# Post-LN decoder: the second layer's key/value side re-cut and moved to pairs 5 to 7, the VectorE division moved behind the second clamp and the score slot

## The chip, the cores and the metric

One core of one Trainium2 chip. The metric is the device time of one execution in microseconds; the kernel before has a median of 1208.59 us over 3 runs (1207.61 to 1209.77).

## The reference, cut to what matters

Two decoder layers over `x` (8 batches of 256 rows of 128) with a context `ctx_1024` (8 batches of 512 rows of 128). The first layer is a windowed self-attention with 16 heads of 8, a cross-attention with 16 heads of 64 (rotary keys, scores clipped to ±11) and a quantised product. The second layer is a recurrence over 256 steps, a linear cross-attention and an fp8-like product. What the change touches is the division of the first layer's cross-attention and the key/value side of the second layer's:

```python
# first layer, cross-attention
attn = softmax(clip(q @ k.T * scale, -11, 11))      # 16 heads, in 8 pairs
out  = attn @ v

# second layer, linear cross-attention: key/value side
kh = _split_heads(_layernorm(ctx @ wk, ln_gamma, ln_beta))     # eps 1e-6
vh = _split_heads(_layernorm(ctx @ wv, ln_gamma, ln_beta))
k_prime = (relu(kh) + 1e-6) * mask
vh = vh * mask
kv = einsum('bhnd,bhne->bhde', k_prime, vh)          # and k_prime.sum over the rows
```

Only the 128 by 128 product of `k_prime` with `vh`, and the column sums of `k_prime`, leave this side; they are kept per batch in `kv_sums`, and the last stage of the kernel reads them.

## The kernel before, in words

The program has a queue of its own for each engine, and each queue is written out in the order in which it executes; the engines meet through semaphores.

**Three parts.** First a setup with the self-attention of batch 0, for which no other work runs beside it (0 to about 87 us). Then a loop over the batches b = 0 to 7, in each of which the cross-attention of batch b runs as 8 pairs of heads, and the self-attention of batch b+1 is dealt out between its steps in 48 slots, 6 to a pair (`PER_PAIR`, `S_...`, lines 57 to 67; slot s belongs to pair s // 6). The last batch has pairs without slots. Then the rest of both layers, from about 868 us on: the recurrence and what follows, which the change leaves alone but for the width of one tile.

**A pair.** TensorE (`batch` under `block.tensor`, `unit` at line 1572): `unit(0)` makes half the scores in the two score banks, then the keys' first product for the pair after next, slot 0, then `values_of(pair - 1)` (L1544) and `sum_of(pair - 1)` (L1552) into `out_bank`, slot 1, `unit(1)` into the same score banks, and then the queries' product, slots and the other products ("prep" jobs, L1358 to L1360) in turns. ScalarE: `exps(0)`, slots 0 and 1, `exps(1)` (L776), then queries, slots and values evacuations (L738). VectorE (`batch`, lines 1075 to 1105): `keys_job("a")` (k_cos, L1010), `clamp(0)` (L1078), slots 0 and 1, `attended(pair - 1)` (reciprocal L1050 and product L1051), `clamp(1)`, slot 2, `keys_job("b")` (k_sin, L1012), slots 3 and 4 and 5. GpSimd: slots 0 and 1, two of three additions of the clamped values (L614, L616), slots 2 and 3, the third (L618), slot 4, `rotate` (L590), slot 5.

**What waits for what.** `values_of` of the next pair and, at the end of pair 0, `output` of the batch before (L1527, 32 matmuls) wait for `on_ready`, which `attended` gives. `unit(1)` waits for `exps(0)`, and the `unit(0)` after it for `exps(1)` and the queries' evacuation. The prep jobs go through one or two banks: in pairs 1 and 5 the second values job, in pair 3 (one bank only) the first, waits until `keys_job("b")` has emptied the bank. `bank_a` is a single bank that ScalarE empties, in the order of the jobs `A_X` to `A_LAT` (lines 70 to 71); `bank_d` the same for VectorE. A score slot (L1428) waits until VectorE has read the scores before it (L939, L941).

**The second layer's key/value side, for batch b+1.** Slot 3 (pair 0): TensorE turns the context into `bank_a` (L1339, from `cb`), ScalarE copies it to `ctx_t`. Slots 5 and 6: two products each of 128x256 with `w_l1kv` (L1417), each half copied by ScalarE to `kv1` (L670, 128x512). Slots 9 and 13: VectorE takes mean and variance of four tiles of `kv1` (`measure`, L885, L888), GpSimd makes scale and bias (`scale_and_bias`, L548 to L551). Slots 10 and 15: ScalarE normalises four tiles in place (L678). Slots 17 to 20: GpSimd multiplies by `l1_g` and adds `l1_b`, two halves of 128x512 each (L572). Slot 23: VectorE makes relu, value times mask, key times mask (L960 to L962). Slot 40: TensorE makes the product (L1464, 4 matmuls of 128x129), VectorE copies it (L993).

```python
                if slot in S_NORM:
                    k = S_NORM.index(slot)
                    tiles = tiles_of(kv1[:, KB * k:KB * (k + 1), :], KB)
                    dve.wait_ge(a_free, n(b, ACT_JOBS, SETUP_A + A_KV + k + 1))
                    dve.wait_ge(rstd_ready, norms + 1 + k)
                    measure(tiles, 1)
```

## Time and profile before

| | us |
|---|---|
| median of 3 runs | 1208.59 |
| the profiled execution: time | 1209.53 |
| its span, first to last instruction | 1207.7 |
| setup and self-attention of batch 0 | 0 to 88.2 |
| loop, batches 0 to 6 (with slots), one each | 100.0, 100.5, 100.9, 101.9, 100.0, 101.3, 100.0 |
| last batch (no slots) | 69.4 |
| the rest | 345.5 |
| PE / DVE / ACT / POOL busy | 991.9 (82%) / 686.5 (57%) / 520.4 (43%) / 484.0 (40%) |

Read the stages first: a mean over them says nothing of a change that moves work within one iteration of the loop. A pair's stage is measured here from its first score matmul (`unit(0)`) to the next pair's, so that its length is what TensorE spends on it. PE is TensorE, DVE VectorE, ACT ScalarE, POOL GpSimd.

### The profile page before, as it was taken

What the parts mean: (1) busy time and instruction counts of PE and PEld (TensorE: products, weight loads), DVE (VectorE), ACT (ScalarE), POOL (GpSimd) and SP (SyncE); (2) the same over time, 40 slices, a digit from 0 to 9 for tenths busy, and PEclk for the clock granted to TensorE, in tenths of its full rate; (3) what the DMA queues carried; (4) which work ended last, traced back from release to release, by engine and by line L of the source; (5) the groups of instructions that cost most, each with busy time, mean ns of one, the idle gap of its engine ahead of it and who ended that gap; (6) DMA issues with size and microseconds to landing.
All of it is one profiled execution on the core that took longest, in us unless ns stands there. A gap on an engine that the chain in (4) does not pass through costs nothing.

```text
span 1207.7 us, 19775 instructions
## 1 busy us (share of the span) xinstructions
PE 991.9 (82%) x7491; PEld 664.9 (55%) x7491; DVE 686.5 (57%) x1895; ACT 520.4 (43%) x1414; POOL 484.0 (40%) x553
## 2 busy tenths in 40 slices
PE   4578899899799979989979998998746999996311
PEld 3355566566566656656756665665434755663311
DVE  2535666566656666666765767654474002445498
ACT  3726545564664465556466446532211233331000
POOL 1224555546455554654645555465421000111031
PEclk8779899799999989989998999999956999997655
DMA  6000000000000000000000000000000000010401
GB/s 167 18 3 13 1 1 14 1 1 6 10 1 1 14 2 1 14 1 1 6 10 1 1 1 1 1 19 1 1 1 1 2 1 4 8 8 3 52 0 35
DMA packets 56813, 12.85 MB, mean 11 GB/s; under 512 B 40318, under 2 KB 56462, under 8 KB 56590
## 3 DMA queue, kind: packets, MB, share of 16 engines
q1 hardware_dynamic: 56718, 11.58, 4.7%
q8 instruction: 60, 0.98, 0.3%
q14 instruction: 35, 0.29, 0.1%
HBM read 9.46 MB, written 2.12 MB: 10 GB/s over the span
## 4 chain that ended last, share of the span: by engine, by line
PE 58%; DVE 23%; ACT 10%; POOL 3%; issue 3%; DMA 2%; SPq 1%; POOLq 0%; DVEq 0%
PE score_banks L1572 8%; PE out_bank L1544 8%; PE bank_d L1670 6%; PE bank_a L1339 5%; DVE o_rec L1050 5%; PE score_banks L1734 4%; PE score_banks L1358 4%; DVE prob L1078 3%; ACT prob L716 3%; PE score_banks L1383 3%; DVE stats L885 3%; PE out_bank L1527 3%; PE score_banks L1360 2%; PE score_banks L1359 2%; PE out_bank L1552 2%
## 5 line engine op out<-in xcount | busy, mean ns | idle before, releaser
L776 ACT ACTIVATE prob<-score_banks 128x1024 f32<-128x1024 f32 x128 | 130.8, 1022 | 154.5 <-PE score_banks L1572 154.1
L1572 PE MATMUL score_banks<-qh,kr 64*128 64x256 f32 x1024 | 153.2, 420 | 6.2 <-ACT prob L776 4.9
L616 POOL TENSOR_TENSOR psum<-psum,prob 128x512 f32<-128x512 f32 x64 | 81.6, 1274 | 166.1 <-DVE prob L1078 166.1
L539 POOL TENSOR_TENSOR var_eps<-mv,epsilons 128x2 f32<-128x2 f32 (+2 forms) x64 | 12.6, 197 | 335.6 <-DVE mv L888 335.4
L1050 DVE RECIPROCAL o_rec<-out_bank 128x256 f32<-128x256 f32 x64 | 111.8, 1747 | 32.9 <-PE out_bank L1552 32.9
L1544 PE MATMUL out_bank<-prob,v 128*64 128x256 f32 x1024 | 124.6, 385 | 1.3 <-DVE on L1051 1.3
L614 POOL TENSOR_TENSOR psum<-prob 128x512 f32<-128x512 f32 x64 | 82.3, 1286 | 99.5 <-DVE prob L1078 99.5
L1572 PEld LDWEIGHTS score_banks<-qh,kr 64*128 64x128 f32 x1024 | 92.8, 195 | 45.4 <-issue 26.6
L1078 DVE TENSOR_SCALAR prob<-prob 128x1024 f32<-128x1024 f32 x128 | 101.2, 790 | 26.9 <-ACT prob L776 26.9
L1010 DVE TENSOR_TENSOR k_cos<-score_banks,cos_t 128x512 f32<-128x512 f32 x56 | 38.6, 690 | 123.0 <-POOL kr L590 75.4
L716 ACT ACTIVATE prob<-prob,neg_max 128x128 f32<-128x128 f32 (+1 forms) x256 | 106.4, 420 | 0.0
L1670 PE MATMUL bank_d<-w_qkv_t,ident 128*64 128x192 f32 (+1 forms) x430 | 105.9, 332 | 0.0
L1428 PE MATMUL bank_d<-km,q 64*128 64x128 f32 (+1 forms) x512 | 60.9, 361 | 47.3 <-DVE row_max L941 46.7
L1339 PE MATMUL bank_a<-ident,prob 128*128 128x128 f32 x400 | 73.8, 315 | 27.4 <-DMA prob<-att_scratch 17.4
L1544 PEld LDWEIGHTS out_bank<-prob,v 128*64 128x64 f32 x1024 | 67.8, 136 | 46.8 <-issue 17.4
L827 ACT ACTIVATE prob<-score_banks 128x8 f32<-128x8 f32 x255 | 45.2, 177 | 104.9 <-PE score_banks L1734 103.6
L590 POOL TENSOR_TENSOR kr<-k_cos,k_sin 128x512 f32<-128x512 f32 x64 | 82.8, 1293 | 10.3 <-DVE k_sin L1012 10.3
L618 POOL TENSOR_TENSOR psum<-psum,prob 128x512 f32<-128x512 f32 x64 | 81.5, 1273 | 3.4
L1734 PEld LDWEIGHTS score_banks<-prob,pt 128*64 128x64 f32 x1020 | 52.2, 134 | 54.6 <-ACT prob L827 48.6
L670 ACT ACTIVATE pt<-bank_a 128x512 f32<-128x512 f32 x96 | 57.0, 594 | 55.2 <-PE bank_a L1339 55.2
L1339 PEld LDWEIGHTS bank_a<-ident,prob 128*128 128x128 f32 x400 | 50.9, 158 | 53.0 <-DMA prob<-att_scratch 17.9
L1734 PE MATMUL score_banks<-prob,pt 128*64 128x8 f32 x1020 | 75.3, 212 | 0.7 <-ACT prob L827 0.3
(352 smaller groups left out, 2035.6 us busy)
## 6 DMA issues: line engine op xcount, KB each, us to landing
cb<-in_ctx_dram SPq DMA_DIRECT2D x8, 256.0 KB, 2.9
bias_mask<-bias_scratch SPq DMA_DIRECT2D x1, 1536.0 KB, 7.5
xb<-in_x_dram SPq DMA_DIRECT2D x8, 128.0 KB, 2.2
prob<-in_L_xattn_Wkv_dram SPq DMA_DIRECT2D x1, 1024.0 KB, 6.8
att_scratch<-on SPq DMA_DIRECT2D x16, 64.0 KB, 3.1
prob<-att_scratch SPq DMA_DIRECT2D x2, 512.0 KB, 4.1
out_dram<-v SPq DMA_DIRECT2D x4, 256.0 KB, 2.3
prob<-in_L_xattn_Wq_dram SPq DMA_DIRECT2D x1, 512.0 KB, 8.1
```

What stands on the lines that cost most here:

```text
L590: g.tensor_tensor(kr[:, key % 2, :], k_cos[:, :], k_sin[:, :], ALU.add).then_inc(kr_ready, 1)
L614: link(g.tensor_tensor(psum[:, p % 2, :], pp[:, 0, :], pp[:, 1, :], ALU.add))
L616: link(g.tensor_tensor(psum[:, p % 2, :], psum[:, p % 2, :], pp[:, 2, :], ALU.add))
L716: last = s.activation(pr, pr, ACT.Exp, bias=neg_max[:, qt, j, g:g + 1], accum_out=row_sum[:, qt, j, g:g + 1])
L776: s.activation(prob[:, p % 2, 2 * u:2 * u + 2, :].rearrange("p k (h q) -> p h k q", h=2), sc[:, 0:2, :].rearrange("p h (k q) -> p h k q", ...
L1050: link(w.reciprocal(o_rec[:, :], bank[:, T:2 * T]))
L1078: w.tensor_scalar(pr, pr, float(np.exp(-CLIP)), float(np.exp(CLIP)), ALU.max, ALU.min).then_inc(clamped, 1)
L1339: return nc.tensor.transpose(out_ap, in_ap, ident[0:in_ap.shape[0], 0:in_ap.shape[0]])
L1544: mm(o[DH * h:DH * (h + 1), 0:T], v[:, (q // 2) % 2, kb, lo:lo + DH], prob[:, q % 2, kb, T * h:T * (h + 1)], start=(kb == 0), stop=(kb == ...
L1572: last = mm(sc[:, h, k * T:(k + 1) * T], kr[rows_of, p % 2, kb * P:(kb + 1) * P], qh[rows_of, p % 2, :], start=True, stop=True, skip_group ...
L1670: mm(bank_d2[0:HALF_ROWS, 0:columns], ident[:, 0:HALF_ROWS], w_qkv_t[:, 0:columns], start=True, stop=True, skip_group_check=True)
L1734: last = mm(cf[lo:lo + HALF_ROWS, t * B:(t + 1) * B], a_t[:, lo:lo + HALF_ROWS], hid[:, (t - 1) * B:t * B], start=False, stop=True, skip_g ...
```

## The change

It does two things.

**One.** The second layer's key/value side is computed otherwise. The weights `w_l1kv` are centred once at the start on VectorE (2 statistics, 2 aggregations, 2 subtractions), so that a row of the product has mean zero and needs a scale alone. `kv1` is gone: VectorE measures the product in `bank_a` itself, GpSimd makes the scale (add, power, times a mask factor: 3 operations in place of 4), and ScalarE writes each of the four tiles of a half scaled out of `bank_a` into `k1` or `v1` (4 activations of 128x128 in place of one copy of 128x512 and 4 activations). GpSimd's gain and bias are applied to `k1` alone (2 operations in place of 4), VectorE's relu too (1 in place of 3); the values' gain and bias are applied to the 128x128 product, with one column more in the matmul (128x130) and three VectorE operations in place of one copy.

**Two.** All of it moves: the context's turning from slot 3 to 34, the two halves of the product from slots 5 and 6 to 35 and 39, the statistics with them on VectorE, GpSimd's scale to slots 36 and 40, ScalarE's evacuation to 37 and 41, gain and bias to 42 and 43, relu to 44, the last product from slot 40 to 47. And in every pair `attended` comes behind `clamp(1)` and slot 2.

```diff
-S_X, S_K, S_Q, S_CTX, S_V, S_KV_A, S_KV_B = range(7)
+S_X, S_K, S_Q, S_CTX, S_V = range(5)
-S_CTX_NORM, S_NORM, S_KV_NORM, S_AFFINE, S_RELU = 5, (9, 13), (10, 15), (17, 18, 19, 20), 23
-S_SUMS, S_REC, S_DIVIDE, S_PROJ, S_X1, S_LATN, S_KV, S_LAT = 29, 33, 34, 35, 37, 38, 40, 43
+S_CTX_NORM = 5
+S_SUMS, S_REC, S_DIVIDE, S_PROJ, S_X1, S_LATN, S_LAT = 29, 33, 34, 35, 37, 38, 43
+S_TURN_CTX, S_KV, S_KV_SCALE, S_KV_OUT = 34, (35, 39), (36, 40), (37, 41)
+S_AFFINE, S_RELU, S_KV_SUM = (42, 43), 44, 47
-A_X, A_K, A_CTX, A_KV, A_CN, A_TURN, A_REC, A_LAT = 0, 1, 2, 3, 5, 6, 18, 19
+A_X, A_K, A_CN, A_TURN, A_REC, A_CTX, A_KV, A_LAT = 0, 1, 2, 3, 15, 16, 17, 19
...
 # GpSimd
+                if slot in S_KV_SCALE:
+                    half = S_KV_SCALE.index(slot)
+                    scale = act_scale[:, 1 + half, :]
+                    if half == 0:
...
+                        g.tensor_copy(v1[:, :, D:D + 2], keep_pair[:, b, :, :])
+                    pool.wait_ge(kv_var_ready, n(b, 2, half + 1))
+                    link(g.tensor_tensor(var_eps[:, 4:8], mv[:, 4:8, 1], epsilons[:, EPSILONS.index(1e-6), 4:8], ALU.add))
+                    link(g.tensor_tensor(scale, var_eps[:, 4:8], minus_half[:, 4:8], ALU.pow))
+                    g.tensor_tensor(scale, scale,
+                                    kv_factor[:, b, 2 * half:2 * half + 2, :].rearrange("p k t -> p (k t)"),
+                                    ALU.mult).then_inc(kv_scale_ready, 1)
                 if slot in S_AFFINE:
+                    first = slot == S_AFFINE[0]
+                    if first:
+                        pool.wait_ge(a_free, n(b, ACT_JOBS, SETUP_A + A_KV + 2))
+                    row, op = (l1_g, ALU.mult) if first else (l1_b, ALU.add)
+                    last = g.tensor_tensor(k1[:, :, :], k1[:, :, :], row[:, :].unsqueeze(1).broadcast_to([P, KB, D]), op)
...
 # ScalarE
+                if slot in S_KV_OUT:
+                    half = S_KV_OUT.index(slot)
+                    act.wait_ge(kv_scale_ready, n(b, 2, half + 1))
+                    if half == 0 and b >= 1:
+                        act.wait_ge(d_free, n(b, DVE_JOBS, SETUP_D))
+                    for i in range(4):
+                        dst = (k1[:, 2 * half + i // 2, :], v1[:, 2 * half + i // 2, 0:D])[i % 2]
+                        last = s.activation(dst, bank_a[:, i * D:(i + 1) * D], ACT.Identity,
+                                            scale=act_scale[:, 1 + half, i:i + 1])
+                    last.then_inc(a_free, 1)
-                if slot == S_CTX:
+                if slot == S_TURN_CTX:
+                    act.wait_ge(cn_split, b + 1)
                     evacuate(b, A_CTX, ctx_t[:, :], bank_a[:, :])
-                if slot in (S_KV_A, S_KV_B):
-                    evacuate(b, A_KV + k, kv1[:, 4 * k:4 * k + 4, :].rearrange("p k d -> p (k d)"), bank_a[:, :])
...
 # VectorE
+                if slot in S_KV:
+                    half = S_KV.index(slot)
+                    dve.wait_ge(a_full, n(b, ACT_JOBS, SETUP_A + A_KV + half + 1))
+                    if half == 1:
+                        dve.wait_ge(kv_scale_ready, n(b, 2, 1))
+                    measure(tiles_of(bank_a[:, :].rearrange("p (k d) -> p k d", d=D), 4), 1, kv_var_ready)
                 if slot == S_RELU:
                     dve.wait_ge(kv_ready, n(b, 1, 1))
-                    link(w.tensor_scalar(k1[:, :, :], kv1_v[:, :, 0, :], 0.0, 1e-6, ALU.max, ALU.add))
-                    w.tensor_tensor(v1[:, :, 0:D], kv1_v[:, :, 1, :], keep_b, ALU.mult)
-                    w.tensor_tensor(k1[:, :, :], k1[:, :, :], keep_b, ALU.mult).then_inc(k1_ready, 1)
+                    w.tensor_scalar(k1[:, :, :], k1[:, :, :], 0.0, 1e-6, ALU.max, ALU.add).then_inc(k1_ready, 1)
-                if slot == S_KV:
+                if slot == S_KV_SUM:
                     bank_ready(b, D_KV)
-                    w.tensor_copy(kv_sums[:, b, :], bank_d[:, 0:D + 1]).then_inc(d_free, 1)
+                    w.tensor_copy(kv_sums[:, b, D:D + 2], bank_d[:, D:D + 2])
+                    link(w.tensor_tensor(kv_sums[:, b, 0:D], bank_d[:, 0:D], l1_g[:, :], ALU.mult))
+                    w.scalar_tensor_tensor(out=kv_sums[:, b, 0:D], in0=l1_b[:, :], scalar=kv_sums[:, b, D + 1:D + 2],
+                                           in1=kv_sums[:, b, 0:D], op0=ALU.mult, op1=ALU.add).then_inc(d_free, 1)
...
                     clamp(0)
                     slots(0, 1)
                     slots(1, 2)
+                    clamp(1)
+                    slots(2, 3)
                     if pair >= 1:
                         attended(pair - 1)
-                    clamp(1)
-                    slots(2, 3)
                     keys_job("b")
...
 # TensorE
-                if slot == S_CTX:
+                if slot == S_TURN_CTX:
                     pe.wait_ge(ctx_in, n(b, 16, 16))
                     a_job(A_CTX)
-                if slot in (S_KV_A, S_KV_B):
+                if slot in S_KV:
...
-                if slot == S_KV:
+                if slot == S_KV_SUM:
                     bank = d_job(D_KV)
                     pe.wait_ge(k1_ready, n(b, 1, 1))
                     for kb in range(KB):
-                        last = mm(bank[:, 0:D + 1], k1[:, kb, :], v1[:, kb, :], start=(kb == 0), stop=(kb == KB - 1))
+                        last = mm(bank[:, 0:D + 2], k1[:, kb, :], v1[:, kb, :], start=(kb == 0), stop=(kb == KB - 1))
```

On SyncE the load of the next context follows the context's turning (`a_free` of `A_CTX`), and so moves from pair 0 to pair 5.

## Rows read from the trace of the kernel before

**Rows 1.** Busy time by pair of one iteration: stage, length, PE, PEld, DVE, ACT, POOL, clock

```profile
288.70:302.40 13.70, 13.46 (x98) 10.41 (x97) 8.16 (x19) 6.38 (x13) 9.77 (x11) 1.00 0.04 11
302.40:317.30 14.90, 12.67 (x92) 8.86 (x91) 10.98 (x43) 7.36 (x14) 4.84 (x7) 0.97 0.07 19
317.30:336.80 19.50, 15.12 (x98) 9.46 (x97) 11.02 (x46) 13.24 (x43) 12.84 (x16) 0.76 0.00 1
336.80:351.00 14.20, 13.75 (x119) 9.16 (x118) 9.89 (x25) 8.37 (x25) 8.01 (x7) 1.00 0.00 1
...
361.20:373.10 11.90, 11.90 (x101) 8.39 (x99) 7.05 (x9) 5.54 (x11) 5.97 (x6) 1.00 0.00 0
373.10:380.60 7.50, 7.50 (x56) 5.11 (x55) 6.48 (x16) 2.60 (x4) 4.23 (x7) 1.00 0.01 3
380.60:389.60 9.00, 8.90 (x62) 5.82 (x61) 7.17 (x11) 4.54 (x7) 5.34 (x5) 1.00 0.00 0
```

**Rows 2.** Timeline of pairs 1 and 2: start, duration, engine, line, idle before and releaser

```profile
314.97 0.82 PE L1428 MATMUL bank_d<-km,q 64*128 64x128 f32 x8 [2.09 <-DVE row_max L941]
315.20 0.68 DVE L1012 TENSOR_TENSOR k_sin<-score_banks,sin_t 128x512 f32<-128x512 f32 x1
...
317.26 2.08 PE L1572 MATMUL score_banks<-qh,kr 64*128 64x256 f32 x8
...
319.11 1.65 ACT L678 ACTIVATE kv<-kv,act_bias,act_scale 128x128 f32<-128x128 f32 x4 [5.58 <-POOL act_bias L551]
...
328.80 1.68 DVE L1078 TENSOR_SCALAR prob<-prob 128x1024 f32<-128x1024 f32 x1
...
331.60 1.44 PE L1428 MATMUL bank_d<-km,q 64*128 64x128 f32 x8 [3.91 <-DVE row_max L941]
```

**Rows 3.** Busy time of lines over that iteration: count, busy us, mean ns, idle before

```profile
L1050 DVE RECIPROCAL o_rec<-out_bank 128x256 f32<-128x256 f32 x8 | 14.0, 1747 | 3.9 <-PE out_bank L1552 3.9
L1078 DVE TENSOR_SCALAR prob<-prob 128x1024 f32<-128x1024 f32 x17 | 13.5, 792 | 2.7 <-ACT prob L776 2.7
...
L572 POOL TENSOR_TENSOR kv<-kv,l_g 128x512 f32<-128x512 f32 x2 | 2.5, 1272 | 0.1
...
L678 ACT ACTIVATE kv<-kv,act_bias,act_scale 128x128 f32<-128x128 f32 x8 | 3.3, 482 | 7.3 <-POOL act_bias L551 7.3
...
L549 POOL TENSOR_TENSOR act_scale<-var_eps,minus_half 128x4 f32<-128x4 f32 x3 | 3.1, 1017 | 0.2
...
L1417 PE MATMUL bank_a<-w_l1kv,ctx_t 128*128 128x256 f32 x8 | 2.2, 392 | 0.2 <-ACT ctx_t L670 0.2
...
L885 DVE BATCH_NORM_STATS2 stats<-kv 128x6 f32<-128x128 f32 x8 | 1.7, 276 | 0.0
...
L1464 PE MATMUL bank_d<-v,k 128*128 128x129 f32 x8 | 1.1, 274 | 0.0
```

**Rows 4.** Timeline of pairs 0, 3, 5, 6 and 7 around the division

```profile
294.98 1.02 ACT L776 ACTIVATE prob<-score_banks 128x1024 f32<-128x1024 f32 x1 [0.69 <-PE score_banks L1572]
...
298.71 0.49 PE L1527 MATMUL out_bank<-wo,on 128*128 128x128 f32 x3
...
343.57 1.02 ACT L776 ACTIVATE prob<-score_banks 128x1024 f32<-128x1024 f32 x1 [3.30 <-PE score_banks L1572]
...
347.42 0.39 PE L1358 MATMUL score_banks<-wv_s,cn_s 128*128 128x256 f32 x1 [0.24 <-DVE k_sin L1012]
...
370.44 0.69 DVE L1012 TENSOR_TENSOR k_sin<-score_banks,sin_t 128x512 f32<-128x512 f32 x1 [0.68 <-PE score_banks L1360]
...
378.56 1.03 ACT L776 ACTIVATE prob<-score_banks 128x1024 f32<-128x1024 f32 x1 [3.24 <-PE score_banks L1572]
...
385.23 1.13 PE L1572 MATMUL score_banks<-qh,kr 64*128 64x256 f32 x8
```

**Rows 5.** Chain that ended last, before the loop: start, duration, engine, line

```profile
69.41 0.73 PE bank_d L1456 x4
...
78.43 0.77 PE score_banks L1358
```

More of the change, by code:

```diff
@@ L279, in decoder @@
         x2 = sb("x2", [P, NT, D])
-        kv_sums = sb("kv_sums", [P, B, D + 1])
+        kv_sums = sb("kv_sums", [P, B, D + 2])
         mats = km[:, :, :].rearrange("p j t -> p (j t)").rearrange("p (k d) -> p k d", d=D)
@@ L542, in rstd_of, with scale_and_bias @@
                                 ALU.pow).then_inc(done, 1)
-            def scale_and_bias(before, k, eps):
-                scale, bias = act_scale[:, k, :], act_bias[:, k, :]
-                pool.wait_ge(var_ready, before + k + 1)
-                link(g.tensor_tensor(var_eps[:, 4:8], mv[:, 4:8, 1], epsilons[:, EPSILONS.index(eps), 4:8], ALU.add))
+            def scale_and_bias(before):
+                scale, bias = act_scale[:, 0, :], act_bias[:, :]
+                pool.wait_ge(var_ready, before + 1)
+                link(g.tensor_tensor(var_eps[:, 4:8], mv[:, 4:8, 1], epsilons[:, 0, 4:8], ALU.add))
                 link(g.tensor_tensor(scale, var_eps[:, 4:8], minus_half[:, 4:8], ALU.pow))
@@ L672, in evacuate, with apply_norm @@
                     i.then_inc(a_free, 1)
-            def apply_norm(norms, k, dst, src):
-                act.wait_ge(rstd_ready, norms + k + 1)
-                for i in range(4):
-                    last = s.activation(dst[:, i, :], src[:, i, :], ACT.Identity, scale=act_scale[:, k, i:i + 1],
-                                        bias=act_bias[:, k, i:i + 1])
+            def apply_norm(norms):
+                act.wait_ge(rstd_ready, norms + 1)
+                for i in range(KB):
+                    last = s.activation(cn[:, i, :], cb[:, i, :], ACT.Identity, scale=act_scale[:, 0, i:i + 1],
+                                        bias=act_bias[:, i:i + 1])
                 return last
@@ L875, in _ @@
             w.tensor_copy(cos_t[:, :], bank_d[:, :]).then_inc(d_free, 1)
+            for half in range(2):
+                w.bn_stats(stats[:, half, :], w_l1kv[:, half * D:(half + 1) * D])
+            link(w.memset(stats[:, 2, 0:1], 0.0))
+            for half in range(2):
+                w.bn_aggr(mv[:, half, :], stats[:, half, :])
+            link(w.memset(stats[:, 2, 0:1], 0.0))
+            for half in range(2):
+                tile = w_l1kv[:, half * D:(half + 1) * D]
+                last = w.tensor_scalar(tile, tile, mv[:, half, 0:1], None, ALU.subtract)
+            last.then_inc(kv_centred, 1)
             def band_of(h, count):
@@ L1411, in self_attention @@
                     last.then_inc(d_full, 1)
-                if slot in (S_KV_A, S_KV_B):
-                    j = slot - S_KV_A
+                if slot in S_KV:
+                    j = S_KV.index(slot)
+                    if b == 0:
+                        pe.wait_ge(kv_centred, 1)
                     a_job(A_KV + j)
```

69 lines of the change are left out of this document (28 added, 41 removed).

## The prediction

> **What bounds the kernel now.** I read the busy time by pair first [rows 1]. Seven of the 48-slot iterations make up 705 of the 1207.7 us, so the question is what one of them becomes. In pairs 5 to 7 (and in pair 4, left out of the rows) TensorE is busy for the whole stage at full clock: these are bound by its work. Pairs 1 and 2 are not: pair 2 takes 19.5 us for 15.12 of TensorE, at a granted clock of 0.76, and 15.12 x 0.76 = 11.5 is what it would need at full clock. The timeline says why [rows 2]: TensorE waits 2.09 and 3.91 us for VectorE to read scores, and ScalarE waits 5.58 us for GpSimd's scale of the key/value side before its four activations, with the exponentials of pair 2 queued behind them. So an iteration has slack of two kinds: TensorE's idle time in pairs 1 and 2, which the change attacks, and VectorE's and ScalarE's idle time in pairs 4 to 7, which it wants to use. The second kind is worth something only if the new steps there don't form a chain that TensorE waits for.
>
> **The change part by part**, for one iteration, each number against the lengths of [rows 1].
>
> *Pair 2, 19.5 to 12.2: -7.3.* The chain measure (1.3: four statistics of 0.28 overlapping, four aggregations), GpSimd's four operations (1.9, of which the power is 1.02 [rows 3]), ScalarE's 1.65 [rows 2] leaves the path to the first exponential; a second measure of 1.3 leaves VectorE, and the slot's scores come ahead of the division, so that the 3.91 us wait goes. I take TensorE's own 11.5 plus 0.7 of leftover waits.
>
> *Pair 1, 14.9 to 14.0: -0.9.* Half the product leaves (2.2 us for both halves [rows 3], 0.9 of queue pace each). The wait of 2.09 us changes its cause instead of going: the second values job needs `k_sin` out of its bank, and k_sin stood at 315.20, the job right behind it [rows 2]. VectorE still has to do the exponential's clamp, the scores, the division and k_sin in a row, after the second exponential, whose time is TensorE's doing. I get k_sin at the same time after the stage's start, within 0.4.
>
> *Pair 0, 13.7 to 14.1: +0.4.* The other half of the product and the turning leave (1.3). But the second exponential ends at 296.0 [rows 4]; the division (a reciprocal of 1.75 [rows 3] and a product, 2.2 in all) used the wait for it and was over by then. Now it comes behind it: clamp 0.7, slot 2's scaling of the queries 0.4, division 2.2, so 299.4 with the starts. TensorE's output of the batch before, which needs this division, began at 298.71 [rows 4] and, with 1.3 us less ahead of it, could begin at 297.4. It waits 2, and ends 0.4 later than before after all; the GpSimd and VectorE steps behind it have their 2 us of idle time to take that in.
>
> *Pair 3, 14.2 to 16.4: +2.2.* The same, with a price one can read off: the first values job waits for k_sin already now (0.24 at 347.42, rows 4), k_sin follows the division, and the division leaves the gap in front of the exponential that ends at 344.6. It shifts by its whole 2.2. That GpSimd's four additions and VectorE's mask products (3.8 us at the pair's end) go is worth nothing: they ran beside TensorE's work, and k_sin was ahead of them.
>
> *Pair 4: 0.* k_sin is late by 1.7, but its bank is needed in pair 5 only.
>
> *Pair 5, 11.9 to 13.5: +1.6.* Turning 0.45 and half a product 0.9 come in; k_sin moves from 370.44 [rows 4] to about 372.0, which delays the second values job by 0.3.
>
> *Pairs 6 and 7, 16.5 to 24.2: +7.7.* The heart of the matter. Time runs from pair 6's first score matmul. VectorE measures half A (1.3) ahead of the projection's sum, so GpSimd has done the projection's scale only at 3.3 and half A's (a copy and three operations, 1.9) at 5.2; ScalarE's four activations (4 x 0.41 = 1.65) stand ahead of the second exponential and end at 6.9, so that one ends at 7.95 (was 6.5: 378.56 + 1.03, rows 4). Call this E. From there one chain has to run before the first exponential of pair 7, which is queued on ScalarE behind half B's activations: clamp 0.7, latent norm 0.6, division 2.2, k_sin 0.7, measure B 1.3, GpSimd 1.7, ScalarE 1.65, exponential 1.05: E + 10. Pair 7's `unit(1)` starts at 17.9; it started at 12.1 (385.23, rows 4). That is +5.8. Then TensorE has values 1.5, and needs GpSimd's gain and bias (2 x 1.27 [rows 3]) and relu for the last product; relu sits behind the second clamp and ends 3.6 after `unit(1)`'s start; product 1.05 [rows 3], queries 0.55, keys 0.9, in all 6.2 against 4.4. +1.9. TensorE idles some 5 us in this stretch. The turning of the latents waits as well, since it needs `bank_a` from half B; it is ready before `unit(1)` all the same.
>
> *The clock: +2.* After the idle 2.09 us the eight score matmuls of pair 2 took 2.08 against 1.13 us elsewhere [rows 2, 4], and the stage shows 0.76 [rows 1]; the granted clock was at its lower level, 1.2 GHz. One such stretch costs TensorE about 1.7 us. My lengths for pairs 1 and 2 assume full clock, which takes out what they lost; but there are now idle stretches of 2 us or more in pairs 0, 1, 3 and 7. Between 0 and 4 x 1.7 = 6.8; in the trace not each wait of 2 us was followed by a fall, so I take 2.
>
> Sum: -7.3 - 0.9 + 0.4 + 2.2 + 1.6 + 7.7 + 2 = +5.7 for an iteration, times 7: **+40**.
>
> *Ahead of the loop: +8.* Two passes of ScalarE's four activations (3.2) leave the chain of exponentials. But between the projection (69.41) and the first prep job (78.43) [rows 5] ran 9.0 us of latents; now both halves of the key/value side, A, then B, then gain, bias, relu and product run there, with nothing beside them: from the projection's old time 1.7 (half A ahead of it), 1.3 measure, 2.2 the projection's sum and scale, 2.5 GpSimd, 1.65, half B 0.9 + 1.3 + 1.7 + 1.65, and 5 for gain, bias, relu and product: 20 in place of 9.0, and 20 - 9 - 3.2 = 7.8. Centring the weights (some 1.6 us) hides in VectorE's idle time before 17 us.
>
> *Last batch: +11.* No slots, so pairs are short, and the division's 2.2 us comes right before what needs it: it ends 2.9 after the second exponential (clamp 0.7, division 2.2), where the next pair's values can start 2.0 after it (scores 1.1, keys 0.9), and k_sin is 2.2 later where a values job waits for it. Pair 0 3.2 (the output, with a clock loss); pairs 1, 3 and 5, where the wait is for k_sin, 2.1, 1.0 and 1.9, the second less as TensorE's keys are late there already; pairs 2, 4 and 6 0.6, 0.6 and 1.5; the last division 1.2, as GpSimd's sum was late already. Of these 12 I take 11.
>
> *At nothing:* the one column more in the matmul, the load of the context (needed only at the next pair 0), three VectorE operations for `kv_sums` (1.0 in place of 0.3, beside GpSimd's rotation, for which VectorE waits there).
>
> **A rule beside the rows.** The clamp took 1.68 us at 328.80 [rows 2] against a mean of 0.79 [rows 3]; GpSimd's addition L614 ran beside it. The Trainium skill (SBUF — State Buffer, the shared port pair) has it that VectorE and GpSimd take that pair in turns for a whole instruction, the loser blocked. By that the two additions and the mask products saved would free VectorE, which speaks for the change; and relu and clamp of pair 7 would meet GpSimd's additions, which were ahead of them, which speaks against it by 0.8 to 1 us an iteration. My sum has neither.
>
> **It comes to** 1209.5 (the profiled execution; its span is 1207.7) + 40 + 8 + 11 = 1268.5; the median is 0.9 below that execution: **1267.6 us**.
>
> **The rivals.** (a) *Faster.* VectorE and ScalarE get to the division and to half B in time, and only the gain of pairs 0 to 3 stands: then these need TensorE's work alone, by busy time times clock in [rows 1] 51.0, less the 2.2 moved 48.8, in place of 62.3 us. With pairs 5 to 7 at my price (+9.3) that is -4.2 an iteration: 1208.6 - 29 + 8 + 11 = 1199; were only the 2.2 us of moved work added there, 1208.6 - 79 + 19 = 1149. For it: VectorE idles a third of the iteration. Against: the waits are for one instruction in a fixed order, and the exponential's end is TensorE's doing, not VectorE's. The point from which it decides is half B's last activation: done by 11.0 us after pair 6 began it delays nothing (12.1 less an exponential); I sum 17. The queue order is the same in every iteration, so it would be all seven or none. 0.10. (b) *Half hidden.* The chain from E is 3 to 4 us shorter than summed (its waits overlapping with what I put behind one another): 21 to 28 us less, about 1240 to 1247; 0.2. (c) *All idle stretches lose the clock*: +4.8 an iteration, 1301; also if SBUF contention adds: 0.12. (d) *No change.* The gain in pair 2 larger by 3 and the chain shorter by 3, about 1212 to 1205: 0.03. (e) The move does not take place, since something ties the slots: no; each queue is written in order. My forecast itself has 0.55.
>
> **How the numbers follow.** Over 0.2% (about what a measurement of this kernel can tell from no change) slower are the forecast, (b) and (c): 0.87. The range: no clock loss (-14) and (b) together give 1226, and I go some way on towards (d), to 1218, as (a) and (d) lie outside with 0.13; above, (c) gives 1300.
>
> **What would show it.** Right: pair 2 near 12 us and the wait before ScalarE's activations gone there; ScalarE waiting 2 us and more for GpSimd's scale in pairs 6 and 7, and the first exponential of pair 7 about 10 us after the second of pair 6; a wait of TensorE's output for the division in pair 0; in pair 3 a wait of 2 us for k_sin; iterations of about 106 us. Wrong: pairs 6 and 7 together under 19 us, or pairs 0 to 3 together under 52.

## The result, and the profile after

The changed kernel takes **1272.9 us** (median of 4 runs, 1269.43 to 1276.43) against 1209.18 for the kernel before beside it: **1.053 times as long, 95% interval 1.0506 to 1.0557**. It was forecast at 1267.6, in a range of 1218 to 1300, and slower with 0.87. The profiled execution spans 1268.4 us, so 60.7 have to be found against the 1207.7 of before. VectorE, ScalarE and GpSimd are busy for less than before (682.5, 504.8 and 467.7 us), and TensorE's work is the same but for its clock.

Busy time by pair of the iteration that answers to [rows 1]; its columns are stage, length, then PE, PEld, DVE, ACT and POOL busy with their counts, granted clock, DMA share and GB/s:

```profile
300.10:314.40 14.30, 12.11 (x88) 9.23 (x87) 9.46 (x21) 4.68 (x9) 6.40 (x10) 1.00 0.04 11
314.40:328.30 13.90, 11.34 (x86) 7.74 (x85) 10.62 (x40) 8.27 (x18) 7.96 (x8) 1.00 0.00 1
328.30:341.70 13.40, 11.79 (x101) 7.64 (x99) 8.41 (x34) 9.41 (x31) 5.53 (x5) 1.00 0.01 2
341.70:358.00 16.30, 13.72 (x121) 9.14 (x119) 7.07 (x23) 8.49 (x26) 5.09 (x4) 1.00 0.01 1
...
368.10:381.80 13.70, 13.70 (x112) 9.77 (x109) 7.48 (x12) 6.42 (x12) 6.81 (x6) 1.00 0.02 5
381.80:389.20 7.40, 7.40 (x50) 4.75 (x49) 4.94 (x21) 3.36 (x7) 4.97 (x10) 1.00 0.10 31
389.20:407.40 18.20, 12.80 (x68) 8.47 (x67) 13.49 (x21) 5.46 (x11) 12.45 (x12) 0.82 0.00 0
```

Pair 2 went from 19.5 to 13.4 us and back to full clock; pair 7 doubled, with 5.4 us in which TensorE does nothing, at a granted clock of 0.82. Iterations differ by some us, so I count with the mean of each pair over batches 0 to 6 from here on:

| us | before | after | difference |
|---|---|---|---|
| pair 0 | 12.92 | 13.69 | +0.8 |
| pair 1 | 15.23 | 14.32 | -0.9 |
| pair 2 | 19.33 | 13.44 | -5.9 |
| pair 3 | 14.88 | 16.32 | +1.4 |
| pair 4 | 10.17 | 10.17 | 0 |
| pair 5 | 11.94 | 13.61 | +1.7 |
| pairs 6 and 7 | 16.46 | 24.46 | +8.0 |
| sum, times 7 batches | | | +36 |
| first pair starts | 86.29 | 93.79 | +7.5 |
| from batch 7's pair 0 to the end | 414.9 | 432.4 | +17.5 |

36 + 7.5 + 17.5 = 61: that is the whole difference (60.7, unrounded). The timeline of pairs 6 and 7 shows the chain (pair 6 begins at 381.76):

```profile
386.72 0.37 ACT L710 ACTIVATE k<-bank_a,act_scale 128x128 f32<-128x128 f32 x1 [2.75 <-POOL act_scale L583]
...
387.74 1.04 ACT L797 ACTIVATE prob<-score_banks 128x1024 f32<-128x1024 f32 x1
...
388.81 1.32 DVE L1108 TENSOR_SCALAR prob<-prob 128x1024 f32<-128x1024 f32 x1 [2.22 <-ACT prob L797]
...
390.05 1.59 DVE L931 TENSOR_SCALAR lat<-x,mv,rstd 128x128 f32<-128x128 f32 x2
...
391.57 1.74 DVE L1080 RECIPROCAL o_rec<-out_bank 128x256 f32<-128x256 f32 x1
391.64 1.26 POOL L636 TENSOR_TENSOR psum<-psum,prob 128x512 f32<-128x512 f32 x1
393.35 0.42 DVE L1081 TENSOR_TENSOR on<-out_bank,o_rec 128x256 f32<-128x256 f32 x1
393.69 0.68 DVE L1044 TENSOR_TENSOR k_sin<-score_banks,sin_t 128x512 f32<-128x512 f32 x1
...
393.82 3.45 PE L1576 MATMUL out_bank<-prob,v 128*64 128x256 f32 x16 [2.58 <-DVE on L1081]
...
397.26 0.37 ACT L710 ACTIVATE k<-bank_a,act_scale 128x128 f32<-128x128 f32 x1 [8.21 <-POOL act_scale L583]
...
399.37 1.13 PE L1604 MATMUL score_banks<-qh,kr 64*128 64x256 f32 x8 [0.47 <-ACT prob L797]
...
403.90 1.67 PE L1496 MATMUL bank_d<-v,k 128*128 128x130 f32 x8 [1.77 <-DVE k L991]
```

Read it from ScalarE: it waits 2.75 us for the scale of half A and 8.21 for that of half B, and `unit(1)` of pair 7 starts behind it at 399.37, 17.6 us after pair 6 began (it was 12.1 before, [rows 4]). TensorE has a second wait of its own, 2.58 us at 393.82, for the division, and the sixteen value matmuls behind it take 3.45 us. The same sixteen take 1.95 where the clock is granted in full, as in the next fence. The other waits for VectorE, in pairs 0, 1 and 3 and in the last batch's last two value steps and output:

```profile
310.66 3.84 PE L1559 MATMUL out_bank<-wo,on 128*128 128x128 f32 x32 [2.19 <-DVE on L1081]
327.45 0.38 PE L1388 MATMUL score_banks<-wv_s,cn_s 128*128 128x256 f32 x1 [2.28 <-DVE k_sin L1044]
354.39 0.38 PE L1388 MATMUL score_banks<-wv_s,cn_s 128*128 128x256 f32 x1 [2.37 <-DVE k_sin L1044]
...
913.76 1.95 PE L1576 MATMUL out_bank<-prob,v 128*64 128x256 f32 x16 [1.40 <-DVE on L1081]
921.18 3.68 PE L1576 MATMUL out_bank<-prob,v 128*64 128x256 f32 x16 [3.98 <-DVE on L1081]
928.03 6.16 PE L1559 MATMUL out_bank<-wo,on 128*128 128x128 f32 x30 [2.32 <-DVE on L1081]
```

Why VectorE is late though it works less stands in one row of the costliest groups, the clamps. They wait 165.9 us for the exponentials in the whole kernel:

```profile
L1108 DVE TENSOR_SCALAR prob<-prob 128x1024 f32<-128x1024 f32 x128 | 102.5, 801 | 165.9 <-ACT prob L797 165.1
```

The row of the kernel before, for the same 128 clamps:

```profile
L1078 DVE TENSOR_SCALAR prob<-prob 128x1024 f32<-128x1024 f32 x128 | 101.2, 790 | 26.9 <-ACT prob L776 26.9
```

The other 139 us of waiting were filled by the division, done while VectorE would have waited anyway. The experiments below bear this out: the same row shows 21.4 us of waiting with the division back in its place (experiment 1) and 157.8 with the division alone moved (experiment 2).

### The profile page after: what moved, and what is told of

It reads as the page before. It is cut to its first block, busy times and chain, and to the rows that moved or that the text cites. A ratio compares the mean times of both kernels' runs of the same rounds, so it can differ in the third digit from the quotient of the medians.

```text
span 1268.4 us, 19745 instructions
## 1 busy us (share of the span) xinstructions
PE 990.2 (78%) x7491; PEld 664.3 (52%) x7491; DVE 682.5 (54%) x1903; ACT 504.8 (40%) x1398; POOL 467.7 (37%) x532
## 4 chain that ended last, share of the span: by engine, by line
PE 53%; DVE 25%; ACT 11%; issue 4%; POOL 3%; DMA 2%; SPq 1%; POOLq 0%; DVEq 0%; ACTq 0%
PE score_banks L1604 8%; PE out_bank L1576 7%; PE bank_d L1702 6%; DVE o_rec L1080 6%; ACT prob L797 5%; PE bank_a L1369 4%; PE score_banks L1766 4%; PE out_bank L1559 3%; PE score_banks L1388 3%; DVE stats L917 3%; DVE prob L1108 3%; PE score_banks L1413 2%; ACT prob L737 2%; PE out_bank L1584 2%; PE score_banks L1390 2%
## 5 line engine op out<-in xcount | busy, mean ns | idle before, releaser
L1108 DVE TENSOR_SCALAR prob<-prob 128x1024 f32<-128x1024 f32 x128 | 102.5, 801 | 165.9 <-ACT prob L797 165.1
L1576 PE MATMUL out_bank<-prob,v 128*64 128x256 f32 x1024 | 136.0, 412 | 24.5 <-DVE on L1081 24.5
L1604 PE MATMUL score_banks<-qh,kr 64*128 64x256 f32 x1024 | 148.0, 408 | 5.0 <-ACT prob L797 3.7
L1604 PEld LDWEIGHTS score_banks<-qh,kr 64*128 64x128 f32 x1024 | 89.9, 189 | 44.1 <-issue 29.3
L1576 PEld LDWEIGHTS out_bank<-prob,v 128*64 128x64 f32 x1024 | 71.9, 144 | 75.1 <-DVE on L1081 29.2
L1369 PE MATMUL bank_a<-ident,prob 128*128 128x128 f32 x400 | 66.7, 291 | 25.5 <-DMA prob<-att_scratch 17.2
L636 POOL TENSOR_TENSOR psum<-psum,prob 128x512 f32<-128x512 f32 x64 | 81.3, 1270 | 4.5
L1369 PEld LDWEIGHTS bank_a<-ident,prob 128*128 128x128 f32 x400 | 46.3, 146 | 47.6 <-DMA prob<-att_scratch 17.7
L1388 PE MATMUL score_banks<-wv_s,cn_s 128*128 128x256 f32 x112 | 36.8, 328 | 40.1 <-DVE k_sin L1044 39.1
```

Source lines behind the costliest of these rows:

```text
L1108: w.tensor_scalar(pr, pr, float(np.exp(-CLIP)), float(np.exp(CLIP)), ALU.max, ALU.min).then_inc(clamped, 1)
L1369: return nc.tensor.transpose(out_ap, in_ap, ident[0:in_ap.shape[0], 0:in_ap.shape[0]])
L1576: mm(o[DH * h:DH * (h + 1), 0:T], v[:, (q // 2) % 2, kb, lo:lo + DH], prob[:, q % 2, kb, T * h:T * (h + 1)], start=(kb == 0), stop=(kb == ...
L1604: last = mm(sc[:, h, k * T:(k + 1) * T], kr[rows_of, p % 2, kb * P:(kb + 1) * P], qh[rows_of, p % 2, :], start=True, stop=True, skip_group ...
```

## The experiments

The change has two parts that can be undone apart. **Theory A**: each has a price, the division's place where TensorE waits for the division or for `k_sin`, the key/value side's place in pairs 6 and 7. **Theory B**: most of it is the chain of the key/value side alone. Each kernel was timed beside the kernel before.

**1. The division back in its place, the rest of the change kept**

```diff
                     slots(1, 2)
+                    if pair >= 1:
+                        attended(pair - 1)
                     clamp(1)
                     slots(2, 3)
-                    if pair >= 1:
-                        attended(pair - 1)
```

> The changed kernel with the division back ahead of the second clamp; the key/value side stays in pairs 5 to 7. Theory A (two prices: the division's place and the late key/value chain, each with its own): the waits for the division in pair 0 and for k_sin in pair 3 go (2.2 us each), pair 5 loses 0.4, pairs 6 and 7 fall from 24.5 to about 22 since the division runs in the wait for the second exponential again, and the last batch gets its 16 us back; an iteration takes about 98 us and the whole about 1200. Theory B (the late key/value chain is what makes the kernel slower, the division is mostly hidden): less than 25 us come back, the whole stays above 1245.

1201.52 us, 0.9936 of before (0.991 to 0.9961). Theory A. By pair against the changed kernel: pair 0 -2.6, pair 3 -2.1, pair 2 -1.0, pairs 6 and 7 -1.1, in all -6.9 an iteration; from the last batch on -19.5. Undoing the place of the division gives back 67 us of span, more than the 61 lost. The key/value side as changed is, alone, **6.7 us faster than before** by the spans of the profiled executions, 5.8 by the medians (-1.8 an iteration, +7.8 ahead of the loop, -2 at the end), though half B's chain is all there:

```profile
374.21 0.37 ACT L710 ACTIVATE k<-bank_a,act_scale 128x128 f32<-128x128 f32 x1 [2.75 <-POOL act_scale L583]
...
382.63 0.37 ACT L710 ACTIVATE k<-bank_a,act_scale 128x128 f32<-128x128 f32 x1 [6.09 <-POOL act_scale L583]
...
384.74 2.08 PE L1604 MATMUL score_banks<-qh,kr 64*128 64x256 f32 x8 [0.48 <-ACT prob L797]
```

Pair 6 began at 369.25 here: `unit(1)` of pair 7 starts 15.5 us later, 2.1 less than in the changed kernel, but its eight matmuls take 2.08 us instead of 1.13. Part of what the shorter chain gave went to the clock. Pairs 6 and 7 still take 23.4 us in the mean, 6.9 more than before: in these two pairs the late chain is a real loss, which the 8.7 us gained over pairs 0 to 5 outweigh.

**2. The division late, the key/value side as before**

The same move, in the kernel before.

> The kernel before with the division alone moved behind the second clamp and slot 2. Theory A: pair 3 +2.2, pair 0 +0.7, pair 5 +0.7, pair 6 +0.6, pair 2 shorter by up to 2 as its scores come ahead of the division; some +2 us an iteration and +16 in the last batch, so about 1240. Theory B: within 10 us of the kernel before.

1276.15 us, 1.0579 (1.0536 to 1.0623): the direction of theory A, but 36 us past its number. The division alone costs 66 us of span here, 67 on top of the new key/value side: over the whole kernel the two parts add up, and the loss is the division's. What I had missed is pair 7, +3.7 us with no key/value chain in it, and a clock lost in pair 3 as well (+2.8):

```profile
399.47 3.40 PE L1544 MATMUL out_bank<-prob,v 128*64 128x256 f32 x16 [2.40 <-DVE on L1051]
```

So in the changed kernel, too, the wait for the division in pair 7 would be there without the wait for half B; they lie side by side, and taking away either brings only part. Pairs 6 and 7 take 16.5 us with neither, 20.1 with the division late, 23.4 with the new key/value side and 24.5 with both: here both together cost 2.6 us less than their sum, in pair 0 they cost 2.0 more.

**3 and 4. Half B's activations behind the first exponential of pair 7 (slot 42), with what follows; then with the division back as well**

```diff
-S_SUMS, S_REC, S_DIVIDE, S_PROJ, S_X1, S_LATN, S_LAT = 29, 33, 34, 35, 37, 38, 43
-S_TURN_CTX, S_KV, S_KV_SCALE, S_KV_OUT = 34, (35, 39), (36, 40), (37, 41)
-S_AFFINE, S_RELU, S_KV_SUM = (42, 43), 44, 47
+S_SUMS, S_REC, S_DIVIDE, S_PROJ, S_X1, S_LATN, S_LAT = 29, 33, 34, 35, 37, 38, 44
+S_TURN_CTX, S_KV, S_KV_SCALE, S_KV_OUT = 34, (35, 39), (36, 40), (37, 42)
+S_AFFINE, S_RELU, S_KV_SUM = (43, 44), 44, 47
```

> The changed kernel with half B's activations behind pair 7's first exponential (slot 42), gain and bias at slots 43 and 44, and the latents' turning at slot 44. Theory A: pair 7's second scores no longer wait for half B; they start when the division has let the values through, some 3 to 4 us earlier; the last product then waits for gain, bias and relu, which gives back 1 to 2. Pairs 6 and 7 together 21.5 to 23 in place of 24.5, the whole about 1255 to 1262. Rival: the wait turns into one of the last product for relu of the same length, and nothing is gained (1270).

1318.59 us, 1.0897 (1.0853 to 1.0942): far above the range expected, and above the rival's 1270. The profiled execution is the shortest of the four (1309.04). Pairs 6 and 7 take 28.3 us. The wait for half B's scale did not go, it became a longer one behind it, in the timeline of pair 7:

```profile
407.03 1.95 PE L1576 MATMUL out_bank<-prob,v 128*64 128x256 f32 x16 [2.58 <-DVE on L1081]
...
416.65 1.26 POOL L592 TENSOR_TENSOR k<-k,l_b 128x512 f32<-128x512 f32 x1
417.95 1.47 DVE L991 TENSOR_SCALAR k<-k 128x512 f32<-128x512 f32 x1 [3.83 <-POOL k L592]
...
419.56 2.07 PE L1496 MATMUL bank_d<-v,k 128*128 128x130 f32 x8 [6.07 <-DVE k L991]
```

In slot 44 GpSimd's second operation stands behind two of its additions, which wait for the second clamp; relu waits for it, and behind relu stand the division and `k_sin`.

> As the run before, and the division back ahead of the second clamp. Theory A: pairs 6 and 7 together about 19 to 20, the rest as in the run with the division back; 96 us an iteration, about 1185 in all, faster than the kernel before. Rival: no better than with the division back alone (1200).

1246.37 us, 1.0317 (1.0294 to 1.034), missed by 61 us for the same reason: pairs 6 and 7 take 27.2 us, 3.8 more than in experiment 1, pairs 1 and 2 together 2.4 more.

**5 and 6. Half B one slot earlier, activations in slot 40; then with the division back as well**

```diff
-S_TURN_CTX, S_KV, S_KV_SCALE, S_KV_OUT = 34, (35, 39), (36, 40), (37, 41)
+S_TURN_CTX, S_KV, S_KV_SCALE, S_KV_OUT = 34, (35, 38), (36, 39), (37, 40)
```

> The changed kernel with half B one slot earlier: product and measure at slot 38 (ahead of the division and k_sin), scale at 39, activations at 40. Theory A: ScalarE is done with half B some 4 us earlier, but the division, now behind a measure too, holds the values of pair 6 about 1 us longer, and pair 7's second scores cannot start before them; pairs 6 and 7 together 23.5 to 25 (24.5 before), the whole 1265 to 1277. Theory B (the key/value chain sets pair 7): 3 us less an iteration, about 1252.

1275.63 us, 1.0538 (1.0481 to 1.0595). The total lies in theory A's range, but not by its mechanism, and that is luck: pairs 6 and 7 gained 2.2 us (22.3, where theory A had 23.5 to 25), most of theory B's 3, and pairs 0 to 3, which the edit does not touch, lost 2.9. The traces show where: TensorE is idle in pairs 0 to 3 for as long as in the changed kernel (8.9 and 9.0 us), but the granted clock (length times one less the clock) withholds 4.3 us there in place of 0.8. So this run does not show that half B's place is worth nothing.

> As the run before, with the division back ahead of the second clamp. Theory A: now the chain over half B alone sets pair 7's second scores, and it is shorter by division and k_sin's places: they start at about 13.6 us after pair 6 began in place of 15.5, and the clock is not lost; 2 to 3 us less an iteration than with the division back alone, about 1184. Rival: no change against that run (1201), since something else, such as GpSimd's queue, ends last.

1220.77 us, 1.0088 (1.007 to 1.0106): missed, and 18 us of span slower than experiment 1. Of these, 6 are in pairs 6 and 7 (24.3 us against 23.4), 11 again in pairs 0 to 2 (2.1 us an iteration withheld by the clock, 0.5 in experiment 1). `unit(1)` came earlier (13.7 us after pair 6 began), but the time was handed to the next wait:

```profile
386.82 1.74 DVE L1080 RECIPROCAL o_rec<-out_bank 128x256 f32<-128x256 f32 x1
388.60 0.42 DVE L1081 TENSOR_TENSOR on<-out_bank,o_rec 128x256 f32<-128x256 f32 x1
388.94 0.68 DVE L1108 TENSOR_SCALAR prob<-prob 128x1024 f32<-128x1024 f32 x1
389.54 0.42 DVE L991 TENSOR_SCALAR k<-k 128x512 f32<-128x512 f32 x1
...
390.11 2.07 PE L1496 MATMUL bank_d<-v,k 128*128 128x130 f32 x8 [3.88 <-DVE k L991]
```

Relu (L991) has its input 2.9 us before it starts, but stands behind the division and the second clamp in VectorE's queue.

**7. The new key/value side, the division back in pairs 0, 3 and 6 only** (the edit is shown against experiment 1)

```diff
+                    early = p in (0, 3, 6)
-                    if pair >= 1:
+                    if early and pair >= 1:
                         attended(pair - 1)
                     clamp(1)
                     slots(2, 3)
+                    if not early and pair >= 1:
+                        attended(pair - 1)
```

> The changed kernel with the division back ahead of the second clamp in pairs 0, 3 and 6 only, the last batch too. Theory A: only these three places cost TensorE much in the loop, 2.5, 2.1 and 1.1 us an iteration, some 40 us in all, and in the last batch some 8 of its 17; about 1225. The other pairs keep what they have. Rival: the price is spread over all pairs and less than half of 71 us comes back (above 1240).

1228.66 us, 1.0148 (1.0132 to 1.0164), near the 1225 expected: three of eight places give back 44 of the 71 us. What is left is pair 2 (15.4 us at a lower clock, 12.5 in experiment 1) and the last batch, 9 us longer. Pair 2 is a fourth place that costs, against the expectation; it is made up for in part by pairs 6 and 7, which take 22.3 us here and 23.4 in experiment 1.

**8. The kernel before, with the division late in pair 2 alone**

```diff
-                    if pair >= 1:
+                    early = p != 2 or last
+                    if early and pair >= 1:
                         attended(pair - 1)
                     clamp(1)
                     slots(2, 3)
+                    if not early and pair >= 1:
+                        attended(pair - 1)
```

> The kernel before with the division moved in pair 2 alone (not in the last batch), the one pair that came out shorter when it was moved everywhere (18.65 against 19.33). Theory A: pair 2 shorter by 0.7 to 2 us, 5 to 14 us less in all, 1194 to 1203. Rival: what pair 2 gains goes again in pair 3, no difference.

1205.91 us (9 runs), 0.9965 (0.9952 to 0.9979): faster, by less than expected. Pair 2, where TensorE waited 3.91 us for scores behind the division [rows 2], is the one pair that the move made shorter in the kernel before, and there it is worth 0.8 us.

**9. The smaller key/value side in the old place, the division in its old place**

The gain in pair 2 could come from the work being smaller or from its being gone. This run leaves it in pairs 0 to 3 (the edit is shown against experiment 1; two waits at its new places are left out).

```diff
-S_CN = 7
+S_CN = 11
...
-S_TURN_CTX, S_KV, S_KV_SCALE, S_KV_OUT = 34, (35, 39), (36, 40), (37, 41)
-S_AFFINE, S_RELU, S_KV_SUM = (42, 43), 44, 47
+S_TURN_CTX, S_KV, S_KV_SCALE, S_KV_OUT = 3, (5, 8), (5, 8), (6, 9)
+S_AFFINE, S_RELU, S_KV_SUM = (17, 18), 23, 40
...
-A_X, A_K, A_CN, A_TURN, A_REC, A_CTX, A_KV, A_LAT = 0, 1, 2, 3, 15, 16, 17, 19
+A_X, A_K, A_CTX, A_KV, A_CN, A_TURN, A_REC, A_LAT = 0, 1, 2, 3, 5, 6, 18, 19
```

> The smaller key/value side in pairs 0 to 3 instead of 5 to 7, the division ahead of the second clamp as before. Slots: context turned in 3, products in 5 and 8, GpSimd's scale in 5 and 8, ScalarE's activations in 6 and 9, gain and bias in 17 and 18, relu in 23, last product in 40; the turning of the normalised context moves from slot 7 to 11. Theory A (the change mixes a gain, fewer operations in pair 2, with two costs of its own: the place of the division and the place of the key/value side): this keeps the gain and neither cost. By pair, from the run with the division back: pair 0 11.1 and 1.3 for turning and half a product, pair 1 14.2 and 1.1, pair 2 12.5 to 13, pair 3 14.2, pair 4 10.2, pair 5 11.9, pairs 6 and 7 16.5 as before: about 93 us an iteration in place of 98.9, and the first pair some 8 us earlier: 1145 to 1170 us. Rival B (pair 2 got shorter because the work left it, not because it is smaller; in pairs 0 to 2 ScalarE again waits for GpSimd's scale ahead of the exponentials): pairs 0 to 2 together near 47 as before, 1185 us or more.

1179.09 us, 0.9737 (0.9708 to 0.9766): theory A in kind, short of its number. Pairs 0 to 2 take 41.8 us (47.5 before), pairs 5 to 7 what they took before, 95.1 in all. But the first pair starts at 97.2 us, 10.9 later than before. GpSimd's timeline ahead of the loop says why:

```profile
21.19 0.20 POOL L556 TENSOR_TENSOR act_bias<-act_bias,minus_one 128x4 f32<-128x4 f32 x1
33.27 0.24 POOL L574 TENSOR_TENSOR kv_factor<-keep 128x32 f32<-128x32 f32 x1 [11.88 <-DMA b_ffn<-in_L_ffn_bias_dram]
```

The factor needs the mask alone, but waits for the last of 18 loads that share a semaphore.

**10. Experiment 6 with gain and bias in slots 41 and 42 and relu in 43**

```diff
-S_AFFINE, S_RELU, S_KV_SUM = (42, 43), 44, 47
+S_AFFINE, S_RELU, S_KV_SUM = (41, 42), 43, 47
```

> The division ahead of the second clamp, half B in slots 38 to 40 as in the run that missed, and now gain and bias in slots 41 and 42 and relu in 43, so that on VectorE relu stands ahead of the latents' difference, the division and the second clamp, and on GpSimd both operations ahead of the additions. Theory A (that run lost what it gained because relu stood behind the division and the clamp, so that the last product waited 3.88 us): this wait goes, pairs 6 and 7 take 20 to 21 us in place of 24.3, 1188 to 1200 us. Rival B (the wait is set by GpSimd's work in pair 7 and by the clock, not by relu's place in VectorE's queue, or VectorE now waits in relu ahead of the clamp and delays TensorE's values): pairs 6 and 7 stay at 23 to 25 us, 1212 to 1225 us.

1200.33 us, 0.9927 (0.9909 to 0.9944), at the edge of theory A's range: pairs 6 and 7 went from 24.3 to 21.5 us, and the wait for relu from 3.88 to 2.06. GpSimd's gain and bias start at the same times after pair 6 began as in experiment 6 (13.84 and 15.2 us), relu 2.9 us earlier: its place in VectorE's queue was what experiment 6 had lost on. As a place for the key/value side, pairs 5 to 7 stay worse than pairs 0 to 3.

**11. Experiment 9 with the mask's load ahead of the weights, on its own semaphore**

```diff
+            load(keep[:, :, :], a["mask_BxS2_ff1"].rearrange("b (k p) -> p b k", p=P), slow=True, signal=keep_in)
             col("L0_xattn_ln_ctx_g", CTX_G, signal=ctx_cols_in)
...
-            load(keep[:, :, :], a["mask_BxS2_ff1"].rearrange("b (k p) -> p b k", p=P), slow=True)
...
                         if b == 0:
-                            pool.wait_ge(weights_in, 16 * SETUP_LOADS)
+                            pool.wait_ge(keep_in, 16)
...
                     if first:
+                        if b == 0:
+                            pool.wait_ge(weights_in, 16 * SETUP_LOADS)
```

> The run with the smaller key/value side in the old place, and the load of the mask moved ahead of the weights, with a semaphore of its own. Theory A (that run missed 1145 to 1170 us mainly because ahead of the loop GpSimd waited 11.88 us, to 33.27 us, until the last of 18 setup loads had landed, although it needed the mask alone, so that the first pair began at 97.18 in place of 86.29 us): the wait goes, the first pair begins at 85 to 88 us, all else stays: 1167 to 1171 us. Rival B (ahead of the loop something else ends last, the table of biases or VectorE's score slots): the first pair begins at 94 us or later, 1175 to 1179 us.

**1167.41 us, 0.9651 of before (0.9631 to 0.9672)**, the fastest here, 43 us below the kernel before beside it and 105 below the changed kernel. The first pair starts at 88.8 us, 8.3 sooner than in experiment 9, slightly above the 85 to 88 expected. Its busy time by pair, in the columns of the first fence:

```profile
274.50:288.20 13.70, 13.40 (x96) 10.37 (x95) 8.09 (x19) 6.44 (x13) 9.84 (x12) 1.00 0.04 11
288.20:303.20 15.00, 12.69 (x90) 8.64 (x89) 12.10 (x55) 7.57 (x22) 10.41 (x15) 0.95 0.06 19
303.20:318.00 14.80, 14.17 (x100) 8.93 (x99) 9.60 (x33) 10.68 (x35) 5.65 (x6) 0.82 0.00 1
...
361.80:370.70 8.90, 8.80 (x60) 5.74 (x59) 7.60 (x13) 4.54 (x7) 5.37 (x5) 1.00 0.00 0
```

Pair 2 is 14.8 us in this batch and 13.8 in the mean, against 19.3 before; pair 7 is as short as ever.

**12. Experiment 11 with the division late in pair 2 alone**

```diff
-                    if pair >= 1:
+                    if pair >= 1 and (p != 2 or last):
                         attended(pair - 1)
                     clamp(1)
                     slots(2, 3)
+                    if p == 2 and not last:
+                        attended(pair - 1)
```

> The kernel of the mask loaded first, with the division behind the second clamp and the score slot in pair 2 alone. Theory A (the place of the division is right or wrong by what waits: in pair 2 TensorE waits 1.55 us for the scores that VectorE reads behind the division, and then runs the eight scores of pair 3 in 2.08 instead of 1.13 us; the next values job finds its bank empty long before): pairs 2 and 3 take 1 to 2.5 us less together, 7 to 17 us less than the kernel of the mask loaded first. Rival B (as in every pair, the division behind the clamp only moves the wait to the keys' second part and to the value matmuls of pair 3, whose first values job waits for it): no shorter, 0 to 10 us more.

1173.6 us, 0.97 (0.9674 to 0.9726): no gain, as rival B has it. Here the move costs about 6 us (1167.55 to 1177.26 over five runs, where experiment 11 has 1165.1 to 1171.37), pairs 2 and 3 0.8 us together. A wait that I had not looked for takes the place of the one for the scores:

```profile
313.33 0.68 DVE L1050 TENSOR_TENSOR k_sin<-score_banks,sin_t 128x512 f32<-128x512 f32 x1
...
314.15 0.43 PE L1421 MATMUL score_banks<-pt,vm 128*32 128x128 f32 x8 [1.32 <-DVE k_sin L1050]
```

L1421 weighs the first layer's values into the bank that `k_sin` empties. The wait is there in all seven iterations, and in none of experiment 11. I had looked for the next values job as its user.

## Why the prediction was right

By its own steps, as changes per iteration, against the means above:

- *Pair 2, -7.3*: -5.9. The wait ahead of ScalarE's activations is gone there, and the clock is full. I took one iteration's 19.5 and a length of 12.2; the means are 19.33 and 13.44. The leftover waits were mis-sized: TensorE idles 1.6 us there, where I took 0.7.
- *Pair 1, -0.9*: -0.9, with the wait's cause changed from the scores to `k_sin` (2.28 us at 327.45), as forecast.
- *Pair 0, +0.4*: +0.8, with the output waiting 2.19 us for the division where 2 was forecast.
- *Pair 3, +2.2*: +1.4. The wait for `k_sin` grew from 0.24 to 2.37 us [rows 4], so by 2.1; the mean of before had lost clock in some batches (14.88 against 14.2 in the rows I read).
- *Pair 5, +1.6*: +1.7. *Pair 4, 0*: 0.
- *Pairs 6 and 7, +7.7*: +8.0, in which part of the clock's 2 lies. The chain from E runs in the trace in the order forecast (clamp, latents, division, `k_sin`, measure, GpSimd, ScalarE, exponential) and takes 10.5 us for 10. `unit(1)` at 17.6 us for 17.9 forecast, out of errors that cancel. E came at 7.0 us and not at 7.95: four activations out of `bank_a` took 1.15 us in all, where I took 4 x 0.41 from activations that read SBUF. Behind it VectorE's clamp took 1.32 us and the latents 1.59, where I had 0.7 and 0.6. So the number of this term is in part luck: its first piece was too large and these were too small.
- *The clock, +2*: right in size for the new places. What the granted clock withheld in pairs 0 and 7, length times one less the clock, averages 2.4 us. The price of 1.7 a stretch had no row beside it; the output's 32 matmuls behind a wait took 5.47 us in the last batch of before where 3.73 is their time at full clock. In the whole iteration what the clock withheld fell from 4.9 to 2.7, since pair 2 no longer loses 3.6.
- Sum +5.7, times 7 **+40**: +5.1 and +36. *Ahead of the loop +8*: +7.5.
- *Last batch +11*: **mis-sized, +17.5**. My terms came to 12.1. Pairs 0 to 5 cost 11.8 us against 9.4 forecast (pairs 0 and 3 1.3 more each). The 1.5 put down to pair 6 shows in pair 7's stage, as the wait of 1.40 at 913.76. From pair 7's start to the last output's it took 16.8 us in place of 12.5, so 4.3 more for the 2.7 of that wait and of "the last division 1.2, as GpSimd's sum was late already": the last value matmuls waited 3.98 us for the division before, and then took 3.68 us instead of 1.95. I had no term for a wait there and none for the clock. Output's start to the recurrence's came to 1.2 more.

The forecast of the total is right; its **assignment** was not quite. It called pairs 6 and 7, with the key/value chain, "the heart of the matter", and never added up what the late division costs by itself. Experiments 1 and 2 show that the new key/value side, by itself, ends 6.7 us ahead, and that the late division costs 66 to 67 us with either key/value side: some 48 in the loop beside the new side (53 beside the old), 12 to 20 at the end. In pairs 6 and 7 the chain does end last, the division a part of it: with the division back `unit(1)` starts 2.1 us sooner, the 2.2 that I had counted, and 6.9 of the 8.0 us stay. What my list of waits for pair 7 did not have is TensorE's own wait at 393.82; it is hidden behind half B's in the changed kernel, and costs 3.7 us where half B is not there (experiment 2).

**The shared port.** The prediction left contention out of the sum, at 0.8 to 1 us an iteration against the change. In pair 7 VectorE's second clamp takes 1.76 us (at 401.67) and the latents' difference (L1028, at 400.26) 1.48, both beside GpSimd's operations on 128x512; relu, which I had named, takes 0.41 at 403.35, where it starts while GpSimd waits. Over pairs 6 and 7, in the mean, the four clamps take 4.7 us (3.6 before), the latents' norm 1.8 (1.5) and their difference 1.5 (0.4): 2.5 us an iteration more than before, so the term was too small; how much of it reaches TensorE's path was not measured by itself. Against it stands the relu of before, which took 1.35 us. The trace agrees with what the Trainium skill (SBUF — State Buffer, Who interferes with whom) says of VectorE and GpSimd, that operations of VectorE outside the two-port forms and with at most one SBUF input don't contend: the reciprocal at 391.57 beside GpSimd's L636, `k_cos` at 398.55 beside L592 and the product at 405.46 beside L636 read one input from PSUM and at most one from SBUF, and kept their 1.74, 0.69 and 0.42 us.

**What stays open.** Why the granted clock falls more often in pairs 0 to 3 when pair 7 is re-ordered. It withholds 0.8 us an iteration there in the changed kernel, 4.3 in experiment 5 and 4.2 in experiment 3, with the same idle time of TensorE; with the division back it is 0.5 in experiment 1, and 3.5, 2.1 and 2.2 in experiments 4, 6 and 10. Within each of these two groups the edits leave pairs 0 to 3 as they are, and no run separates a cause. Nor is it shown what could still be had in pair 2 of experiment 11: of its 13.8 us in the mean TensorE needs 11.7 at full clock, is idle for 1.2 and loses 1.0 to the clock.

## What to carry to other kernels

An operation that runs in an engine's wait for another is free only there: look at what the engine waits for next to it (the clamps' 26.9 us) before putting it behind. Moving work into another engine's idle time is free only if its chain of hand-overs, each in a queue with fixed order, is shorter than the distance to the next thing that TensorE needs; here the smaller work in its old place gave 30 us (experiment 9; 43 with the mask loaded first), and in the idle pairs 5 to 7 only 6 to 9 us (experiments 1 and 10). When a wait is taken away, follow the freed buffer to every user, since three of the runs (3, 6, 12) handed their gain to one that was not on the list.
